# First and last FFN of a four-layer network kernel in whole float32 over image pairs, in place of split token and weight parts

## What is computed

```python
def _L0_ffn_ref(x, attention_mask, wr, br, w1, b1, w2, b2):       # b=16, s=256, d=64, w1 64x256
    weights = (jnp.einsum('bsd,do->bso', x, wr) + br)[..., 0]
    _, idx = jax.lax.top_k(weights, k)                            # k = 128, the first 127 are used
    sel = jnp.take_along_axis(x, sel_idx[:, :, None], axis=1)
    h = jax.nn.gelu(jnp.einsum('bkd,dh->bkh', sel, w1) + b1)
    y = jnp.einsum('bkh,hd->bkd', h, w2) + b2
    y = y * w_sel[..., None]
    ...
def _L3_ffn_ref(x, Wr, br, W1, b1, W2, b2, gamma, beta):          # 8 experts, W1 64x128, W2 128x64
    logits = jnp.mean(x, axis=1) @ Wr + br                        # one router decision per image
    ...
    top_w, top_i = jax.lax.top_k(rw_tok, K)                       # 2 experts per image
    h = jax.nn.gelu(jnp.einsum('nd,edf->enf', xf, W1) + b1[:, None, :], approximate=False)
    y = jnp.einsum('enf,efd->end', h, W2) + b2[:, None, :]
    out = jnp.einsum('ne,end->nd', w_dense, y).reshape(B, S, D)
    out = _layer_norm(out + x, gamma, beta)
    return out
```

## Time and profile before

| | |
|---|---|
| Median of 3 runs | 725.32 us (719.83 to 726.35) |
| The profiled execution | 725.44 us, span 723.7 us |
| Busy, share of the span | PE 84%, PEld 54%, DVE 63%, ACT 51%, POOL 36% |
| Chain that ended last | PE 62%, DVE 23%, ACT 6%, issue 4%, POOL 3% |
| Mean granted clock of TensorE | 0.857 of full speed |

### The profile page before, as it was taken

The page is one execution under the profiler, slowest core; times in us unless marked ns, Lnnn a source line. Parts: engine busy times, 40 slices in busy tenths (PEclk is TensorE's granted clock), DMA queues, the critical chain, the costliest instruction groups (busy, mean ns, idle before and its releaser), DMA issues.

```text
span 723.7 us, 11445 instructions
## 1 busy us (share of the span) xinstructions
PE 605.3 (84%) x3354; PEld 394.3 (54%) x3354; DVE 456.5 (63%) x1333; ACT 368.1 (51%) x781; POOL 260.4 (36%) x349
## 2 busy tenths in 40 slices
PE   5778494658999999999978898898999999994384
PEld 3465352546555555555547776696545454463252
DVE  5543979687877787777785577485243333438566
ACT  3233485365644434443436354355666667535384
POOL 6400645170355434543453000171323432335153
PEclk8885697555999999999998899875999999995595
DMA  4800000020734333342501000020422221100001
GB/s 107 155 4 1 2 0 1 0 60 2 163 76 103 82 86 89 79 96 58 117 0 38 1 2 0 1 49 2 123 59 58 80 67 58 30 2 0 2 2 58
DMA packets 24529, 34.57 MB, mean 48 GB/s; under 512 B 10984, under 2 KB 20224, under 8 KB 22368
## 3 DMA queue, kind: packets, MB, share of 16 engines
q1 hardware_dynamic: 24480, 33.95, 19.9%
HBM read 32.50 MB, written 1.44 MB: 47 GB/s over the span
## 4 chain that ended last, share of the span: by engine, by line
PE 62%; DVE 23%; ACT 6%; issue 4%; POOL 3%; DVEq 1%; DMA 0%; ACTq 0%; POOLq 0%
PE ps L1754 13%; PE ps L2319 8%; PE ps L2335 8%; PE ps L1774 6%; DVE ST L485 3%; PE ps L602 3%; PE ps L2439 2%; PE ps L777 2%; PE ps L1350 1%; PE ps L1541 1%; PE ps L2057 1%; PE ps L2035 1%; PE ps L2047 1%; ACT act_buf L1721 1%; PE ps L2059 1%
## 5 line engine op out<-in xcount | busy, mean ns | idle before, releaser
L1452 POOL TENSOR_TENSOR out_acc<-out_acc,tok_tmp 128x512 f32<-128x512 f32 x80 | 103.6, 1295 | 215.4 <-DVE tok_tmp L1669 117.1
L1754 PE MATMUL ps<-tokT,w 128*128 128x512 f32 x512 | 137.1, 415 | 2.6 <-DVE hid_buf L1664 1.3
L1754 PEld LDWEIGHTS ps<-tokT,w 128*128 128x128 f32 x512 | 94.6, 194 | 52.2 <-issue 24.3
L1721 ACT ACTIVATE act_buf<-ps 128x512 f32<-128x512 f32 x128 | 75.7, 595 | 92.3 <-PE ps L1754 89.3
L2319 PE MATMUL ps<-tokT,w 128*128 128x512 f32 x256 | 70.6, 420 | 2.1 <-ACT hid_buf L2298 2.1
L2319 PEld LDWEIGHTS ps<-tokT,w 128*128 128x128 f32 x256 | 47.8, 197 | 29.5 <-ACT hid_buf L2298 14.2
L602 PE MATMUL ps<-ident,tok_split 128*128 128x128 f32 x160 | 34.1, 384 | 33.6 <-DVE tok_split L597 33.6
L1664 DVE TENSOR_TENSOR hid_buf<-act_buf,ps 128x512 f32<-128x512 f32 x64 | 43.4, 685 | 20.2 <-ACT act_buf L1721 15.9
L1664 DVE TENSOR_TENSOR tok_split<-act_buf,ps 128x512 f32<-128x512 f32 x64 | 43.4, 686 | 16.3 <-ACT act_buf L1721 14.7
L530 ACT ACTIVATE U<-X,nmr,rstd 128x64 f32<-128x64 f32 x104 | 36.5, 429 | 23.1 <-POOL nmr L508 18.0
L602 PEld LDWEIGHTS ps<-ident,tok_split 128*128 128x128 f32 x160 | 27.8, 201 | 37.4 <-DVE tok_split L597 23.8
(11 more groups left out here) (471 smaller groups left out, 1142.4 us busy)
## 6 DMA issues: line engine op xcount, KB each, us to landing
disp_all<-disp_dram SPq DMA_DIRECT2D x32, 512.0 KB, 6.2
disp_all<-disp_dram SPq DMA_DIRECT2D x32, 256.0 KB, 3.9
w_raw<-in_L_ffn_w SPq DMA_DIRECT2D x4, 512.0 KB, 8.0
XIN<-in_x SPq DMA_DIRECT2D x4, 256.0 KB, 3.4
w_raw<-in_L_ffn_W SPq DMA_DIRECT2D x2, 512.0 KB, 5.8
out<-XIN SPq DMA_DIRECT2D x4, 256.0 KB, 2.2
fc_raw<-in_L_conv_upfc_w SPq DMA_DIRECT2D x1, 512.0 KB, 4.7
w<-in_L_ffn_w SPq DMA_DIRECT2D x1, 512.0 KB, 10.0
```

The lines of the kernel that those rows point to most:

```text
L1452: pool.tensor_tensor(out_acc[:, :], out_acc[:, :], weighed[p % 2], ALU.add).then_inc(mm["acc"].sem, 1)
L1721: act.activation(act_buf[e % 2][:, :], ps[:, e % 2, :], ACT.Silu).then_inc(mm["act"].sem, 1)
L1754: last = pe.matmul(ps[:, 2 * k + e % 2, :], w12[:, part, k, EXPERT1[e], :], tokT[:, bass.ts(i, CHUNK)], start=(part == 0), stop=(part == 1))
```

## The change

In both FFNs the tokens are no longer split. PE transposes two neighbouring tiles of U in one 128 x 128 transpose, four per group; the result, float32 in tokP, has the even image of each pair in rows 0 to 63 and the odd one in rows 64 to 127, on half as many columns. The first products use row halves: `half(0)` or `half(1)` of the weights and of tokP, each into a bank of its own. In the first FFN hidden(u) is now one group of four images (512 columns) with one half of the hidden units, on both row halves; the router column stands in two neighbouring columns of wr_slide, once per row half, so that one product serves two images (8 products of 256 columns). f1 and wr are not split any more. In the last FFN w1_8 and its two filling steps in the second expert stage go; DVE picks 64 x 128 per image and expert out of w1_8raw, unit order n is 2*expert + image, and the copies of ACT take 64 rows x 256 columns. POOL's additions wait for both normalizations of their group in place of its split. DVE zeroes tsum first.

```diff
@@ f_pool, f_vector, f_weights
                 sl = slice(g * TG, (g + 1) * TG)
-                pool.wait_ge(*m["f_fs"](g + 1))
+                pool.wait_ge(*m["f_xu"](g + 1))
+                pool.wait_ge(*m["f_xd"](g + 1))
                 pool.tensor_tensor(X[:, sl, :], X[:, sl, :], U[:, sl, :], ALU.add).then_inc(m["f_u"].sem, 1)
...
-            ln_vector(dve, m["f_rstd"], m["f_xu"], m["f_fs"], m["f_ft_ps"])
+            for g in range(G):
+                dve.wait_ge(*m["f_rstd"](g + 1))
+                for t in range(TG // 2):
+                    tt = g * TG + t
+                    last = dve.tensor_scalar(U[:, tt, :], X[:, tt, :], rstd[:, tt:tt + 1], nmr[:, tt:tt + 1], ALU.mult, ALU.add)
+                last.then_inc(m["f_xd"].sem, 1)
...
-            wwait(dve, "f1")
-            vlink(dve.tensor_copy(f1[:, 0, :], f1_raw[:, :]))
-            dve.tensor_tensor(f1[:, 1, :], f1_raw[:, :], f1[:, 0, :].bitcast(F32), ALU.subtract).then_inc(s_f1, 1)
             wwait(dve, "wr0")
-            vlink(dve.memset(wr_slide[:, :, :].bitcast(F32), 0.0))
...
+            vlink(dve.memset(wr_slide[:, :], 0.0))
+            for r in range(2):
+                rows = slice(r * C, (r + 1) * C)
+                last = dve.tensor_copy(wr_slide[rows, B - 2 + r:B - 1 + r], wr0[rows, :])
+            last.then_inc(s_wr, 1)
@@ f_scalar
+            def pairs(g):
+
+                act.wait_ge(*m["f_ft_ps"](g + 1))
+                act.activation(tokP[:, g * CHUNK:(g + 1) * CHUNK], ps[:, g % 2, :], ACT.Copy).then_inc(m["f_ft"].sem, 1)
+            ln_norm(act, 0, m["f_rstd"], m["f_xu"])
+            act.wait_ge(*m["t_h_ps"](G))
+            for g in range(G):
+                if g + 1 < G:
+                    ln_norm(act, g + 1, m["f_rstd"], m["f_xu"])
+                pairs(g)
@@ f_tensor
+            def pairs(g):
+
+                pe.wait_ge(*m["f_xu"](g + 1))
+                pe.wait_ge(*m["f_xd"](g + 1))
...
+                for i in range(4):
+                    last = pe.transpose(ps[:, g % 2, i * P:(i + 1) * P], pair(U, g * TG + 2 * i), ident[:, :])
+                last.then_inc(m["f_ft_ps"].sem, 1)
...
-                    for part in range(2):
-                        last = pe.matmul(ps[0:B, 7, 0:PIX], wr_slide[:, part, B - 1 - b:2 * B - 1 - b], cols,
-                                         start=(b == 0 and part == 0), stop=(b == B - 1 and part == 1))
+                pe.wait_ge(*m["f_ft"](g + 1))
+                for q in (2 * g, 2 * g + 1):
+                    last = pe.matmul(ps[0:B, 7, 0:PIX], wr_slide[:, B - 2 - 2 * q:2 * B - 2 - 2 * q], tokP[:, q * PIX:(q + 1) * PIX],
+                                     start=(q == 0), stop=(q == B // 2 - 1))
...
-            ln_tensor(pe, m["f_fs"], m["f_ft_ps"], m["f_ft"], [(m["x1"], G), (m["t_h"], G)], then=logits)
+            for g in range(G):
+                pairs(g)
+                if g >= 1:
+                    logits(g - 1)
+            logits(G - 1)
...
-                    for part in range(2):
-                        last = pe.matmul(ps[:, HID0[j % 2] + hc, :], f1[:, part, hc * P:(hc + 1) * P],
-                                         tokT[:, j * CHUNK:(j + 1) * CHUNK], start=(part == 0), stop=(part == 1))
-                    last.then_inc(m["f_h_ps"].sem, 1)
+            def hidden(u):
+
+                g, hc = u // 2, u % 2
+                for r in range(2):
+                    if u >= 2:
+                        pe.wait_ge(*m["f_h"](2 * (u - 2) + r + 1))
+                    pe.matmul(ps[:, HID0[u % 2] + r, :], f1_raw[half(r), hc * P:(hc + 1) * P],
+                              tokP[half(r), g * CHUNK:(g + 1) * CHUNK], start=True, stop=True).then_inc(m["f_h_ps"].sem, 1)
@@ second expert stage
-                    pool.tensor_tensor(w1_8[:, :, 1, :], w1_8raw[:, :, :], w1_8[:, :, 0, :].bitcast(F32), ALU.subtract).then_inc(m["q_i8lo"].sem, 1)
...
-                        act.activation(w1_8[:, :, 0, :], w1_8raw[:, :, :], ACT.Copy).then_inc(m["q_i8hi"].sem, 1)
@@ i_vector
-                    dve.tensor_copy(w1_pick[n][:, :, :], w1_8[:, bass.ds(e, 1), :, :].rearrange("p e h f -> p (e h) f")).then_inc(m["i_ws"].sem, 1)
...
+                        dve.tensor_copy(w1_pick[i % 2][half(r), k, :],
+                                        w1_8raw[half(r), bass.ds(e, 1), :].rearrange("p e f -> p (e f)")).then_inc(m["i_ws"].sem, 1)
@@ i_scalar
+                for q in range(2):
+                    for r in range(2):
+                        b = 2 * (2 * g + q) + r
+                        last = act.activation(tokP[half(r), (2 * g + q) * PIX:(2 * g + q + 1) * PIX], ps[half(r), g % 2, q * PIX:(q + 1) * PIX],
+                                              ACT.Copy, accum_out=tsum[half(r), b:b + 1])
@@ i_tensor
-                    for part in range(2):
-                        last = pe.matmul(ps[:, HB[n], 0:PIX], w1_pick[4 * (i % 2) + n][:, part, :], cols[:, n // 2, :, :],
-                                         start=(part == 0), stop=(part == 1))
-                    last.then_inc(m["i_h_ps"].sem, 1)
+                    pe.matmul(ps[:, HB[n], 0:PIX], w1_pick[i % 2][half(r), k, :], tokP[half(r), i * PIX:(i + 1) * PIX],
+                              start=True, stop=True).then_inc(m["i_h_ps"].sem, 1)
```

More of the change, by code:

```diff
@@ L329, in build @@
         b2u = sb("b2u", [P, B // 2], region="last")
[L330 removed]
+        w1_pick = [sb(f"w1_pick{i}", [P, 2, H3], region="last") for i in range(2)]
         w2_pick = [sb(f"w2_pick{i}", [P, C], region="last") for i in range(8)]
@@ L1184, in outp @@
                 for hc in range(2):
-                    for jj in range(2):
-                        last = pe.matmul(ps[jj * C:(jj + 1) * C, 4, :], f2[:, hc, :], ffn_hid[(2 * g + jj) % 4][:, hc, :],
+                    for r in range(2):
+                        last = pe.matmul(ps[half(r), 4, :], f2[:, hc, :], ffn_hid[(2 * g + hc) % 4][:, r, :],
                                          start=(hc == 0), stop=(hc == 1))
@@ L1207, in f_tensor @@
                     pe.wait_ge(*m["f_mask"](1))
-                    for half in range(2):
-                        last = pe.transpose(ps[:, 7, half * B:(half + 1) * B], tk[:, half * P:(half + 1) * P], ident[0:B, 0:B])
+                    for h in range(2):
+                        last = pe.transpose(ps[:, 7, h * B:(h + 1) * B], tk[:, h * P:(h + 1) * P], ident[0:B, 0:B])
                     last.then_inc(m["f_mt_ps"].sem, 1)
@@ L2525, in i_vector @@
             wwait(dve, "i8")
-            ln_vector(dve, m["i_rstd"], m["i_u"], m["i_fs"], m["i_ft_ps"])
-            dve.wait_ge(*m["i_ft"](NCHUNK))
+            dve.memset(tsum[:, :], 0.0).then_inc(m["i_zero"].sem, 1)
+            for g in range(G):
+                dve.wait_ge(*m["i_rstd"](g + 1))
+                for t in range(TG // 2):
+                    tt = g * TG + t
+                    last = dve.tensor_scalar(U[:, tt, :], X[:, tt, :], rstd[:, tt:tt + 1], nmr[:, tt:tt + 1], ALU.mult, ALU.add)
+                last.then_inc(m["i_fs"].sem, 1)
+            dve.wait_ge(*m["i_ft"](G))
             dve.tensor_scalar(mean8[:, :], tsum[:, :], 1.0 / PIX, None, ALU.mult).then_inc(m["i_mean"].sem, 1)
@@ L2630, in i_scalar, with pairs @@
         def i_scalar(act):
-            ln_scalar(act, m["i_rstd"], m["i_u"], m["i_ft_ps"], m["i_ft"], sums=tsum)
+            def pairs(g):
+                act.wait_ge(*m["i_ft_ps"](g + 1))
+                for q in range(2):
+                    for r in range(2):
+                        b = 2 * (2 * g + q) + r
+                        last = act.activation(tokP[half(r), (2 * g + q) * PIX:(2 * g + q + 1) * PIX], ps[half(r), g % 2, q * PIX:(q + 1) * PIX],
+                                              ACT.Copy, accum_out=tsum[half(r), b:b + 1])
+                last.then_inc(m["i_ft"].sem, 1)
+            ln_norm(act, 0, m["i_rstd"], m["i_u"])
+            act.wait_ge(*m["i_zero"](1))
+            for g in range(G):
+                if g + 1 < G:
+                    ln_norm(act, g + 1, m["i_rstd"], m["i_u"])
+                pairs(g)
             act.wait_ge(*m["i_l"](1))
```

91 lines of the change are left out of this document (43 added, 48 removed).

## The result

Timed on one chip in turns with the kernel before: 717.8 us (median of 20, 715.36 to 723.7) against 722.0 (median of 20, 719.69 to 729.4). The ratio is 0.9947 (95% interval 0.9924 to 0.9971), so the change saves 3.8 us, between 2.1 and 5.5. The time forecast was 717.5, but from 725.4, which lay 3.4 above the median of these 20 runs. Of the gain forecast, 7.9 us, about half came, and the hit in us is partly luck. The profiled run of the changed kernel took 723.16 us (span 721.4), 2.3 under the one before.

The account below looks back on a forecast made before the run. It took DVE's normalization and top-k as the first FFN's chain, ACT's copies as the last FFN's bound once changed. -5.2 - 2.4 - 0.3 = -7.9 from 725.44 gave 717.5 us, range 712.8 to 722.8.

Parts of the forecast that it names:

- First FFN, up to the logits: Normalization, transposes and router products of the first FFN: DVE gets the logits at 89.1 in place of 94.34, -5.2 us.
- Rival 1: First FFN: PE's dearer products at the lower clock until 90 hold the logits back, 719.7 us; chance 0.18.
- First FFN, behind the logits: Top-k of the first FFN: the same 16.6 us, with the loop of products and GELUs no longer than it; 0.
- the slack of 0.95: First FFN: PE reached the mask transposes 0.95 us before the mask came, covering a first GELU 0.4 later.
- Row halves: First FFN's hidden products: two row halves run side by side, so the new eight records take 1.94 us.
- rival 3: The first FFN's loop ends after the mask, which waits 0.7 to 2 us; 719.0 us, chance 0.13.
- Rival 4: The POOL clash at wencb in the first FFN dissolves, picks and copies come out cheap; -10.5, 715 us, chance 0.12.
- rival 2: Row halves do not run side by side: +6 in the first FFN, +5 in the last; 728.5 us, chance 0.07.
- The switch: PE's extra change of tiling mode each round: 0.15 us each, 4 in the first FFN, 8 in the last.
- Last FFN up to the mean: Last FFN's normalization, bound by ACT's copies at 1.6 a group: mean at 667.4 for 669.81, -2.4 us, bounds -1.2 to -3.0.
- Expert loop: Last FFN behind the mean: shorter picks and products against mode switches, -0.3 us, bounds -1.3 to +1.2.
- The bound on the first two hidden(i): Start of the last FFN's expert loop: 3.82 us becomes 2 x 1.91 at most, a gain of 0 to 0.4.

Follow-up runs that it names:

- first_only: The kernel before with the change in the first FFN only; 714.0 us, ratio to before 0.979 to 0.993.
- late_adds: The changed kernel with POOL's X+U additions of the first FFN waiting for all normalizations; 718.4 us, ratio to before 0.9929 to 0.9985.
- one_half: The changed kernel with both hidden products of a unit in the first FFN on row half 0; 721.2 us in one run.
- half_nosum: The changed kernel with the last FFN's half-row copies taking no sums, so its router works on zeros; 718.4 us in one run.
- sum_full: The changed kernel with two whole-row copies with sums per group in the last FFN, in place of four half-row ones; 711.2 us, ratio to before 0.975 to 0.987.
- best3: sum_full with DVE's constants moved to where it waits for the logits and the iotas ahead of POOL's additions; 710.6 us, ratio to before 0.983 to 0.989.
- best2: The change with whole-row copies with sums, POOL's last two w12 subtractions after the next layer norm's statistics, early GELU table load, X+U additions after all normalizations; 712.8 us.

## Why the prediction was right and where it was wrong

**First FFN, up to the logits: right.** -5.2 forecast, -5.76 measured. DVE's normalizations were to take 6.8 (79.2 to 86.0) and took 6.66; POOL's price per addition was to be 0.96 and is 1.0; the products were to be 0.5 each at full clock, four records take 1.04. The rest is the clock, which rose 3 us after the first transpose for the 4.1 to 4.8 that I took (3.5 in first_only and late_adds). So PE was through with its earlier products in time and started the last transposes 0.1 behind DVE's last normalization, where I had it 0.4 late. Rival 1 fell by that.

**First FFN, behind the logits: 0 forecast, -0.5 in the profile of the change, -0.5 to -1.6 in four others with the same first FFN.** My reason for the 0, that the longer first product stays under the slack of 0.95, did not hold. In first_only, with the same first FFN and the clock at 1.00 all along, PE's last transposes end at 105.03 and the mask at 105.05, so that under 0.1 is left:

```profile
104.38 0.65 PE L1222 MATMUL ps<-ident,ffn_outT 128*128 128x128 f32 x4
104.64 0.41 DVE L1091 SCALAR_TENSOR_TENSOR tk<-tk,wl 16x256 f32<-16x256 f32 x1
```

PE's gap at the table load grew from 0.73 (at 96.90 before) to 1.27, for which I had taken 0.4 of delay; the hidden products behind it take 2.86 for 2.47; and 0.17 comes behind the transposes, as told under "Row halves". At full clock the mask still did not wait for PE. In the profile of the change it did, as rival 3 has it, by 0.64, because the clock fell there as well: 3.69 for 2.86 and 2.75 for 1.94 in the two rows of products behind the gap. Why it fell stays open. Seven other profiles have the same gap of 1.27, and in all of them the clock stayed at 1.00, for example in first_only (gap at 91.57), in

```profile
90.40:98.40 8.00, 6.83 (x26) 2.55 (x28) 7.42 (x26) 7.99 (x15) 3.12 (x3) 1.00 0.00 0
```

the same stretch from wl on as 96 to 104 above. So the gap alone does not make it fall. Where PE is in time, POOL's subtraction against DVE's constants decides: of the four such profiles with this first FFN two have 18.61 and two 17.48 or 17.49. Rival 4 had the right place, and took for a small chance what comes about as often as not.

**Row halves: right.** Eight records in 1.99 for 1.94; rival 2 fell, and its price of +6 in the first FFN was too high too (one_half has the stage 2.8 later than the change). The switch that I weighed against the change at up to 0.15 each has a price that shows, though not in the length of a row. Behind the transposes of back, a 128x128 product followed before, now a 64x128 one follows:

```profile
690.47 0.44 PE L2732 MATMUL ps<-ident,sum_copy 128*128 128x128 f32 x2
690.67 1.20 PE L2712 MATMUL ps<-tokT,w_pick 128*128 128x256 f32 x8
```

and after the change

```profile
689.03 0.44 PE L2778 MATMUL ps<-ident,sum_copy 128*128 128x128 f32 x2
689.39 1.14 PE L2759 MATMUL ps<-tokP,w_pick 64*128 64x256 f32 x8
```

From start to start it is 0.20 before and 0.36 after, and in the first FFN 0.41 (105.11 to 105.52) and 0.58 (107.22 to 107.80). The 0.16 to 0.17 are what I had allowed for. Whether the switch of the form or the whole-float32 product makes them is not shown, since both are new there.

**Last FFN up to the mean: wrong, -2.4 forecast, +0.2 measured.** The step that failed is "I take the same time, since a row's 256 columns set it". The columns do set the copy, 0.38. The group's 1.58 though held three read-outs of 0.20 that ran beside the next copy, and I took it as a price of the copies alone. By alternating the row halves the change makes each copy wait: 2.30 a group. Four groups times 0.72 is 2.9 us, all of it on ACT, which is the bound there. The start was right: ACT's first copy comes 2.25 behind the last variance for 3.47 before, 1.2 earlier, and its wait of 1.35 for PE ahead of the last group is gone too. 2.9 less 1.2 less 1.35 is +0.3, about the +0.2 measured. With 1.55 a group (half_nosum) the mean came 2.8 earlier than before, close to the -2.4 forecast. So the mechanism was right (ACT without a gap is the bound, and is), and a term mis-sized.

**Expert loop: not decided.** -0.3 forecast, -0.6 measured, but from the mean to ACT's last instruction the unchanged loop takes 51.30 in the profile before and 50.10 in first_only, and the changed one 50.07 to 51.55 in twelve profiles. A term of 0.3 is under that. The bound on the first two hidden(i) was wrong: they take 4.50 at the lower clock, not at most 3.82. And a round without a wait, from hidden(i) to hidden(i+1), is 2.45 (689.39 to 691.84) for 2.33, because the 0.16 above outweighs the shorter products. Later on DVE's picks set the pace, 6.39 from one PE wait for them to the next, for 6.41. The w1 splits in the second expert stage show no difference that these runs could tell.

**The sum.** By the marks it is -5.4 to the first expert stage and +0.2 to the mean, -5.2 in all, within the 2.1 to 5.5 of the timing; the loop's -0.6 would make it -5.8. The -5.4 is -5.8 up to the logits, -0.5 to wm and +0.9 behind it: 0.7 for the X addition at 113.46, and 0.2 just ahead of the last variance, in every profile with the changed first FFN, whose cause stays open. For sum_full the marks give -5.8 - 5.6 = -11.4 and the timing -9.5 to -17.8; for best3 -7.1 - 5.5 = -12.6 and -8.2 to -12.6. The time forecast was hit although the 2.4 of the last FFN did not come, because the profiled execution it was counted from lay 3.4 above the median. That is luck as to the number; the gain of the first FFN, the largest term, came by the mechanism forecast.

## What to carry to other kernels

Look at what runs beside each instruction before taking over a group's time for another shape: a price that contains an overlap goes when the pattern goes, here the sums' read-out on alternating row halves. When whole-row copies can give the sums of both halves at once, that is the larger gain. And a step on DVE's critical path that stands within a few tenths of a POOL operation on two tensors had two prices here; move it to a time at which DVE waits anyway rather than moving POOL's work to a later critical stretch.

## What the runs showed of the hardware beyond that

ACT: an instruction that starts at another row than the copy with a sum ahead of it starts only when the sum's read-out is through (0.47 to 0.62 from start to start, 64 rows or 128); one that starts at the same row starts while it runs (0.35 to 0.38, or 0.50 where the read-out itself was late). The exception is the kernel before, whose copy at 659.84 waits as well (0.48) with the same rows, where it goes to the other bank and behind a semaphore. What in ACT makes it wait was not tried. PE: 64x128 products of 512 columns in whole float32 on two row halves overlap almost wholly (1.99 for 3.70). PE's clock: behind the same gap of 1.27 us it fell in one profile (0.79 over 8 us) and stayed at 1.00 in seven. DVE: max and match_replace of the top-k (0.42 and 0.40) kept their length beside POOL's subtractions, while the copy ahead of them went from 0.28 to 0.81 beside an addition (best2).
